# Two-layer attention and MLP kernel: the first MLP's inner sum moved from VectorE to TensorE, output biases from GpSimd to TensorE

## The reference, cut to what matters

```python
def _L0_ffn_ref(x, Win, bin_, W1, b1, W2, b2, Wout, bout):     # M = 64, INNER = 16
    s = jnp.einsum('btd,dm->btm', x, Win) + bin_
    h = jax.nn.relu(s[..., None] * W1 + b1)
    g = jnp.einsum('btmh,mh->btm', h, W2) + b2
    out = jnp.einsum('btm,md->btd', g, Wout) + bout
    return out
...
x = x + ga * _L0_attn_ref(...)
x = x + gb * _L0_ffn_ref(h, ...)          # bias bout
x = x + ga * _L1_attn_ref(h, ..., L1_attn_bo)   # bias bo
x = x + gb * _L1_ffn_ref(h, ..., L1_ffn_b2)     # bias b2
```

## Time and profile before

| what | before |
|---|---|
| time, median of 3 runs | 4289.97 us (4288.56 to 4294.81) |
| the profiled execution, first to last instruction | 4290.7 us |
| PE busy | 3633.3 us, 85% |
| PE weight loads busy | 2042.8 us, 48% |
| DVE busy | 2510.6 us, 59% |
| ACT busy | 1932.9 us, 45% |
| POOL busy | 1495.8 us, 35% |
| mean granted clock of PE | 0.914 of full |

### The profile page before, as it was taken

The page is one execution under the profiler, slowest core; times in us unless marked ns, Lnnn a source line. Parts: engine busy times, 40 slices in busy tenths (PEclk is TensorE's granted clock), DMA queues, the critical chain, the costliest instruction groups (busy, mean ns, idle before and its releaser), DMA issues. The chain is left out here.

```text
span 4290.7 us, 59366 instructions
## 1 busy us (share of the span) xinstructions
PE 3633.3 (85%) x19241; PEld 2042.8 (48%) x19241; DVE 2510.6 (59%) x6732; ACT 1932.9 (45%) x4521; POOL 1495.8 (35%) x1807
## 2 busy tenths in 40 slices
PE   7378779987899879998799978998899988998787
PEld 2245444554446534465445544465444644455433
DVE  6754757366663667446573666536674575736652
ACT  5123435545254444554355542544445543545433
POOL 4133441254323451234422543234512444235311
PEclk8589899999899989997999988999899988999888
DMA  6210230002300231002300023002310023001120
GB/s 233 70 33 13 58 104 14 13 27 56 92 16 22 53 81 42 14 12 60 102 14 24 21 55 87 15 22 53 88 34 15 12 60 102 14 24 30 46 65 6
DMA packets 230687, 203.85 MB, mean 48 GB/s; under 512 B 11457, under 2 KB 212417, under 8 KB 230346
## 3 DMA queue, kind: packets, MB, share of 16 engines
q1 hardware_dynamic: 226338, 190.51, 15.9%
q0 software_dynamic: 3328, 8.39, 0.7%
q10 hardware_dynamic: 720, 1.15, 0.1%
HBM read 121.73 MB, written 77.69 MB: 46 GB/s over the span
## 5 line engine op out<-in xcount | busy, mean ns | idle before, releaser
L2330 ACT ACTIVATE arena<-pb 128x512 f32<-128x512 f32 (+3 forms) x1536 | 671.5, 491 | 342.6 <-PE pb L1565 337.5
L2410 POOL TENSOR_TENSOR arena<-arena,small 128x512 f32<-128x512 f32 x256 | 288.0, 1127 | 463.4 <-DVE small L1740 462.0
L2159 ACT ACTIVATE arena<-arena,small 128x256 f32<-128x256 f32 x512 | 256.0, 500 | 394.9 <-DVE small L1723 388.3
L2574 POOL TENSOR_SCALAR_AFFINE_SELECT arena<-arena 128x256 f32<-128x256 f32 x512 | 220.5, 433 | 544.7 <-ACT arena L2330 542.6
L1582 PE MATMUL pb<-arena,v 128*17 128x512 f32 (+3 forms) x3072 | 365.7, 506 | 32.9 <-POOL arena L2574 24.1
L2014 DVE TENSOR_REDUCE arena<-pb 128x1 f32<-128x512 f32 x512 | 329.8, 682 | 90.6 <-PE pb L1540 89.7
L1565 PE MATMUL pb<-arena 98*128 98x512 bf16 (+3 forms) x1152 | 355.3, 343 | 9.4 <-ACT arena L2330 5.7
L1723 DVE CUSTOM_DVE_ANT_0 arena<-pb,wmask 128x256 f32<-128x256 f32 x512 | 195.8, 419 | 218.5 <-PE pb L1282 218.3
L1282 PE MATMUL pb<-arena 128*128 128x256 f32 x1024 | 283.0, 401 | 5.4 <-issue 4.0
L1259 PE MATMUL pb<-hTf,wqkv 128*128 128x512 f32 (+1 forms) x640 | 245.8, 536 | 22.6 <-DVE hTf L1692 10.8
L1660 PE MATMUL pb<-xh,w1T 128*128 128x512 f32 x512 | 251.8, 640 | 9.7 <-DVE xh L1880 8.6
(11 more groups left out here) (354 smaller groups left out, 7588.8 us busy)
## 6 DMA issues: line engine op xcount, KB each, us to landing
arena<-split_q SPq DMA_DIRECT2D x64, 384.0 KB, 4.3
arena<-split_k SPq DMA_DIRECT2D x24, 768.0 KB, 7.1
split_q<-arena SPq DMA_DIRECT2D x64, 192.0 KB, 2.3
split_q<-arena SPq DMA_DIRECT2D x96, 128.0 KB, 2.0
split_k<-arena SPq DMA_DIRECT2D x64, 192.0 KB, 2.4
split_k<-arena SPq DMA_DIRECT2D x96, 128.0 KB, 2.1
arena<-split_k SPq DMA_DIRECT2D x24, 384.0 KB, 5.7
xn<-h_d SPq DMA_DIRECT2D x8, 1024.0 KB
```

The costliest lines, as they stand in the source:

```text
L2159: ins = s.activation(pm[n % 3][:, j], sm[n % 2][:, j], ACT.Exp, bias=nmx[:, 2 * sl + j:2 * sl + j + 1], scale=-1.0, accum_out=sml[:, 2 * s ...
L2330: s.activation(pp[pn % 4][:, h % 2, 0:w_], bank[n % 3][:, 0:w_], ACT.Exp).then_inc(a_exp1, 1)
L2410: g.tensor_tensor(pm[n % 3], pm[n % 3], rcl[:, 2 * sl:2 * sl + 2].unsqueeze(2).broadcast_to([P, 2, 2 * P]), ALU.mult).then_inc(p_norm0, 1)
L2574: g.affine_select(out=p2, in_=p2, pattern=[[0, 2], [1, P]], compare_op=ALU.is_ge, fill=0.0, base=0, channel_multiplier=-1).then_inc(p_tri, 1)
```

## The change

It does five things. The diff below is cut to its core, in the order setup, PE, DVE, ACT, POOL.

1. A constant `w2d` holds eight diagonal 128 x 128 matrices, one for each column of W2. PE multiplies them with the eight Relu results and sums in PSUM (line 1497 of the changed kernel); ACT takes the sum out with the bias b2 (`gt`, line 2312). Lane buffers `rl` grow from two to eight. The eight multiply-adds and the fill of gT on DVE are gone. ACT issues two Relu in a step.
2. A chain has 36 steps in place of 42: four for the sum in place of eight and more, and behind the projection to v six steps in place of eight before the transposes.
3. The biases bout, bo and b2 enter through an extra matmul that starts the group: `ones3` (three rows of ones) times `biasw`, the bias in three bfloat16 parts. There are 2 in each chain, 4 in each `att` half and 4 in each `mlp1` half. The bias additions on POOL are gone.
4. The setup gains their making on POOL: `w2d`, and three parts of 128 x 768 values with copies, subtractions and masks, ahead of the power for the layernorm of sample 0; and one transfer.
5. `PACE` of `att(b, 0)` rises from 1.79, 0.9, 0.72 to 2.09, 1.05, 0.84 steps a round. The mask `wmask` becomes bfloat16.

```diff
-    "hrows": 16, "heavy": 58, "chain": 42, ("mlp1", 0): 24, ("mlp1", 1): 24, "hnorm": 10,
+    "hrows": 16, "heavy": 58, "chain": 36, ("mlp1", 0): 24, ("mlp1", 1): 24, "hnorm": 10,
-PACE = {('light', 0): (1.88, 0.9), ('light', 1): (1.0, 1.1), ('att', 0): (1.79, 0.9, 0.72), ('att', 1): (1.0, 1.15, 0.72)}
+PACE = {('light', 0): (1.88, 0.9), ('light', 1): (1.0, 1.1), ('att', 0): (2.09, 1.05, 0.84), ('att', 1): (1.0, 1.15, 0.72)}
...
+                g.tensor_tensor(w2d[:, :, :], ident[:, :].unsqueeze(1).broadcast_to([P, INNER // 2, P]),
+                                cols[:, C_W2:C_W2 + INNER // 2].unsqueeze(2).broadcast_to([P, INNER // 2, P]), ALU.mult).then_inc(p_w2d, 1)
+                g.wait_ge(in_bias, 16)
+                for k in range(3):
+                    if k:
+                        g.wait_ge(p_part, 2 * k)
+                    g.tensor_copy(bias_part[k], bias_raw).then_inc(p_part, 1)
+                    g.wait_ge(p_part, 2 * k + 1)
+                    g.tensor_tensor(bias_raw, bias_raw, bias_part[k], ALU.subtract).then_inc(p_part, 1)
+                g.wait_ge(p_part, 6)
+                for k in range(3):
+                    g.tensor_tensor(bias_part[k], bias_part[k], ident[:, k:k + 1].broadcast_to([P, 3 * D]), ALU.mult).then_inc(p_part, 1)
...
+                g.tensor_tensor(bw, bias_part[0], bias_part[1], ALU.add).then_inc(p_part, 1)
+                g.tensor_tensor(bw, bw, bias_part[2], ALU.add).then_inc(p_part, 1)
...
                 for _ in gpsimd_hnorm(g)(0, 0):
                     pass
...
-                    for _ in range(9):
-                        yield
+                    yield
+                    bk = chain_bank(c, j, "g")
+                    for k in range(INNER // 2):
+                        t.wait_ge(a_chain[j], nth(CHAIN_A, n, f"l{k}"))
+                        mm = t.matmul(bank[bk][:, 0:2 * P], w2d[:, k, :], L.rl[k], start=k == 0, stop=k == INNER // 2 - 1)
+                        if k == INNER // 2 - 1:
+                            mm.then_inc(t_chain[j], 1)
+                            left[bk] = [(a_chain[j], nth(CHAIN_A, n, "gt"))]
+                        if k % 2:
+                            yield
...
-                    t.wait_ge(v_chain[j], nth(CHAIN_V, n, "g8"))
+                    t.wait_ge(a_chain[j], nth(CHAIN_A, n, "gt"))
                     for i in range(2):
-                        mm = t.matmul(bank[bk][:, i * D:(i + 1) * D], L.gT[:, i * P:(i + 1) * P], wfo[:, :], start=True, stop=True)
+                        t.matmul(bank[bk][:, i * D:(i + 1) * D], ones3[:, :], biasw[:, ROW_BOUT, :], start=True, stop=False)
+                        mm = t.matmul(bank[bk][:, i * D:(i + 1) * D], L.gT[:, i * P:(i + 1) * P], wfo[:, :], start=False, stop=True)
...
-                    for _ in range(8):
+                    for _ in range(6):
                         yield
...
+                        t.matmul(bank[bk][:, 0:D], ones3[:, :], biasw[:, ROW_BO, :], start=True, stop=False)
+                        t.matmul(bank[bk][:, 0:D], ones3[:, :], biasw[:, ROW_B2, :], start=True, stop=False)
...
-                    v.tensor_copy(L.gT, cols[:, C_B2:C_B2 + 1].broadcast_to([P, 2 * P])).then_inc(done, 1)
-                    for k in range(INNER // 2):
-                        v.wait_ge(a_chain[j], nth(CHAIN_A, n, f"l{k}"))
-                        v.wait_ge(done, nth(CHAIN_V, n, f"g{k}"))
-                        v.scalar_tensor_tensor(out=L.gT, in0=L.rl[k % 2], scalar=cols[:, C_W2 + k:C_W2 + k + 1], in1=L.gT,
-                                               op0=ALU.mult, op1=ALU.add).then_inc(done, 1)
+                    for _ in range(8):
                         yield
                     scale(0)
-                    yield
                     add(1)
                     yield
                     scale(1)
-                    yield
...
-                        if k >= 2:
-                            s.wait_ge(v_chain[j], nth(CHAIN_V, n, f"g{k - 1}"))
-                        s.activation(L.rl[k % 2], L.sT, ACT.Relu, scale=cols[:, C_W1 + k:C_W1 + k + 1], bias=cols[:, C_B1 + k:C_B1 + k + 1]).then_inc(done, 1)
-                        yield
+                        s.activation(L.rl[k], L.sT, ACT.Relu, scale=cols[:, C_W1 + k:C_W1 + k + 1], bias=cols[:, C_B1 + k:C_B1 + k + 1]).then_inc(done, 1)
+                        if k % 2:
+                            yield
+                    s.wait_ge(t_chain[j], nth(CHAIN_T, n, "g"))
+                    s.activation(L.gT, bank[chain_bank(c, j, "g")][:, 0:2 * P], ACT.Identity, bias=cols[:, C_B2:C_B2 + 1]).then_inc(done, 1)
+                    yield
...
-                g.tensor_tensor(x, x, bias.unsqueeze(1).broadcast_to([P, 2, D]), ALU.add).then_inc(done, 1)
-                    add_bias(b, c, rows[:, R_B2:R_B2 + D], gates[:, 3])
```

More of the change, by code:

```diff
@@ L45 @@
 NCOLS = 40
-R_NULL, R_BOUT, R_BO, R_B2 = (i * D for i in range(4))
-R_GB = 4 * D
+R_NULL, R_GB = 0, D
 NROWS = R_GB + 4 * HD1
+ROW_BOUT, ROW_BO, ROW_B2 = range(3)
 UNITS = TH * H0 // 2
@@ L145, in turn @@
             return
-        if key[0] == "chain" and key[2] == 3 and n == 41 and not reached([(("chain", key[1], 2), 42), (("att", key[1], 0), 22)]):
+        if key[0] == "chain" and key[2] == 3 and n == STEPS["chain"] - 1 and not reached([(("chain", key[1], 2), STEPS["chain"]), (("att", key[1], 0), 22)]):
             return
@@ L235, in chain_bank @@
     banks = CHAIN_BANKS[c, j]
-    return banks[CHAIN_T.index(op) % len(banks)]
+    turns = [o for o in CHAIN_T if o != "g"]
+    return banks[turns.index("wfo" if op == "g" else op) % len(banks)]
 def nth(ops, n, op):
@@ L369, in adaln_kernel @@
         xh = sb("xh", [P, KD * NH])
-        gbias = sb("gbias", [P, 2, D])
+        w2d = sb("w2d", [P, INNER // 2, P])
+        biasw = sb("biasw", [P, 3, D], BF16)
+        ones3 = sb("ones3", [P, P], BF16)
         small = sb("small", [P, 640])
@@ L700, in adaln_kernel @@
         wtmp = [at(arena, 16384 + F1 * i, [F1]) for i in range(2)]
+        bias_raw = at(arena, 18432, [3 * D])
+        bias_part = [at(arena, 18432 + 3 * D + 3 * D // 2 * i, [3 * D], BF16) for i in range(3)]
         TURNS = [(m, c0, min(4, BINARY[m][1] // P - c0)) for m in range(FT + KD) for c0 in range(0, BINARY[m][1] // P, 4)]
@@ L1171, in __init__ @@
                 view = zone(arena, z)
-                self.sT, self.rl, self.gT = view([2 * P]), [view([2 * P]) for _ in range(2)], view([2 * P])
+                self.sT, self.rl, self.gT = view([2 * P]), [view([2 * P]) for _ in range(INNER // 2)], view([2 * P])
                 self.xpair = view([2, D])
@@ L1672, in mlp1 @@
                                 t.wait_ge(a_g, FT * H + k + 1)
-                            mm = t.matmul(bank[bk][:, 0:D], g1[:, k, i * P:(i + 1) * P], w2T[:, k], start=k == 0, stop=k == FT - 1)
+                            mm = t.matmul(bank[bk][:, 0:D], g1[:, k, i * P:(i + 1) * P], w2T[:, k], start=False, stop=k == FT - 1)
                             if k == FT - 1:
@@ L2299, in chain @@
                     yield
-                    for _ in range(5):
+                    for _ in range(3):
                         yield
@@ L2692, in put_rows @@
                                          L.parts[i][:, m0 + m].unsqueeze(1).broadcast_to([P, n_rows, 2 * P])).then_inc(split_out[c][j], 16)
-                    for _ in range(38):
+                    for _ in range(32):
                         yield
@@ L2810 @@
         "ones": np.full((KA - KS, G1 * N), 0x3F803F80, np.uint32).view(f32),
-        "wmask": np.where(np.stack([first, band, last], 1), 0, NEG).astype(f32),
+        "wmask": (np.where(np.stack([first, band, last], 1), 0, NEG).astype(f32).view(np.uint32) >> 16).astype(np.uint16).reshape(P, 6 * P).view(f32),
         "cmask": np.where(i[None] > i[:, None], NEG, 0).astype(f32),
```

95 lines of the change are left out of this document (41 added, 54 removed).

## The result

The changed kernel took 4390.23 us (median of 4 runs, 4383.63 to 4394.87), the kernel before beside it 4290.6: a ratio of 1.0231, 95% interval 1.0217 to 1.0244. That is 99.6 us slower, where +61 was forecast. Its profiled execution has a span of 4393.1 us, which lies 2.9 us above the median (that of before lay 0.7 above).

What follows compares the result with a forecast made beforehand. PE, busy 85% of the span, was taken as the fullest engine. Terms summed to +6.2 a sample, +50 over eight, plus setup +11: +61 on 4290.7, giving 4351 us, range 4255 to 4415.

Steps and rivals of the forecast that it cites:

- D: Before the first fill: PE's wait for split q and k goes, 58 us in all, about 7.3 a sample.
- C: Second window-attention half: diagonals and bias rows less filled waits, +6.7 a sample; PE waiting at the chains' tails, net +9.7.
- The sign of being right: PE's wait for the last rotation step before the chain's transposes rises from 22.4 to over 100 us, nearly all beside window attention.
- A: Diagonal matmuls in the chains: 512 records at 0.226, 116 us of PE, 14.5 a sample, half beside the window attention.
- E: First half of layer-1 attention: added PE work against waits for DVE and low-clock time given back, net -4.5 a sample.
- B: Bias rows: 192 bfloat16 matmuls at 0.13 us on PE, 25 us, 3.1 a sample.
- F: Elsewhere: 12 bias rows a sample in the MLP halves and second attention half, where PE is full, +1.6.
- G: Setup, once: POOL's new work of 22.3 us delays the layernorm's power, which DVE awaits, +11 us.
- Split k still awaited (D fails): Sign of being wrong: PE still waits for split k at the first fill, so D fails.
- Rival one: The clock comes back in the first attention half: E is -12, C's net half, 4252 us; 20%.
- Rival two: The chains' tails are covered, DVE being less slowed by POOL: C's net about 2, 4290 us, no change; 13%.
- Rival three: PE pays in full in the first attention half, low clock staying: E is +8.2, 4453 or about 4400 us; 15%.

Runs made afterwards that it cites:

- Run 1: Changed kernel, but SyncE starts the loads of split q and k after the window attention's last scores, not its last output product: 4341.13 us.
- run 2: Kernel before the change, with SyncE's loads of split q and k started after the window attention's last scores: 4267.62 us.
- Run 3: Changed kernel with the two steps between v and the chain's transposes restored (chains of 38 steps): 4335.63 us.
- run 4: Changed kernel with the inner sum on DVE again, chains of 42 steps, old pace; bias rows, setup and bfloat16 mask kept: 4304.54 us.
- run 6: Changed kernel, chains 0 and 1 summing on DVE (42 steps), chains 2 and 3 on PE (38), early loads, POOL's setup work behind the power: 4266.62 us.

## Why the prediction was right, and where it was not

The direction, the stated range, and the case that was given 52% (4310 to 4410) were right. The size was 39 us short, and one term of the sum was off by more than that.

**D failed.** The forecast took away 7.3 us a sample at the first fill because the stores come sooner. They do: the last one is issued 26.4 us ahead of the fill where it was 20.2. But the prediction read who was late (the load of split k) and then asked what comes before it in the data, the stores, instead of what the issue itself waited for. The issue times decide: 2484.00 in the kernel before, at the end of the last L1313, 14 us behind the last store. Run 1 shows the cause, run 2 that the same holds before the change. The stretch to the fill went from 10.4 to 10.6: an error of 7.5 a sample, 53 in seven. In the first sample, where the stores are late, the step was right (22.8 to 10.5), and that sample came out at -2.5 instead of +6.2.

**C, the tail, was right** in mechanism and nearly in size. PE stood still for 7.04 us against 7.8 at chain 0, and for 3.54 behind it, where 2.3 was forecast. PE's idle time in the second half rose by 8.3 us a sample; the forecast's +9.7, less the 1.0 of small waits filled, is 8.7. Run 3 gives back 6.6 in that half, and 1.5 in the attention half, where the forecast had no such term. The sign of being right was read from a wrong row: the 22.4 us are 8.4 for the last rotation step (L1967) and 13.9 for L1984, which empties the bank of the transposes. The wait for the rotation went from 8.4 to 88.9, 82.7 of it beside the window attention, where over 100 was named.

**A was right in size and wrong in place.** Chain 0's diagonal matmuls stand in the first half, not the second: PE has 16 of their records (3.9 us) there. Hence +4.2 in the first half, which was forecast to gain only bias rows, and +11.9 in the second instead of 16.4. By run 4 against run 3 the sum costs 7.4 in both, against the 7.2 less 1.0 of the forecast.

**E** came out at -2.7 instead of -4.5. PE's idle time there fell by 4.5 (17.0 to 12.5), where 5.7 was forecast. Its busy time rose by 1.8, where +8.2 - 7 was: the time at the low clock fell from 28.9 to 22.0 us a sample, which at half speed is some 3.5, half of the 7 that I gave back for it, and 8 of the diagonal records stand ahead of the fill. The reason given, DVE's relief from 16 multiply-adds, is right in part at most. Run 4 has the full 2.7 with all of them still on DVE, 2.3 of idle time among it. What relief and pace gave beyond that (2.2 more of idle time, and the low clock from 27.0 to 22.0) paid for the diagonal matmuls there and no more. **B and F** were somewhat high: a row costs 0.11, not 0.13, and about half of them are covered.

**G** was +11 and measured +5.3. In POOL's timeline of the changed kernel the power stands at 163.00, where the earlier trace rows have 156.57:

```profile
162.53 0.40 POOL L1057 TENSOR_TENSOR ones<-ones,ident 128x128 bf16<-128x128 bf16 x1
163.00 1.04 POOL L773 TENSOR_TENSOR small<-small,mhalf 128x4 f32<-128x4 f32 x1
```

That is 6.4 later, not 11: the new work took 19.1 us and not 22.3 (two of the three casts over 128x768 took 0.82 us, the width gave 1.76), and began 1.4 earlier. DVE waited 3.5 of it; most of the rest is DVE slowed beside POOL (L907, 2.4 us more in its four instructions), which the forecast did not have.

Added up, 7 x 14.1 - 2.5 + 5.3 = 101.5 is the difference of the spans, 102.4, within the rounding. Against the forecast the seven samples are 55 us over, of which D is 53; the first sample is 9 and the setup 6 under. That the terms without D sum to +13.5 a sample and measured 13.9 is partly luck: by stretches they were off by +3.7 in the first half, -4.5 in the second, +1.8 in the attention and -0.6 in the rest.

Of the other signs named, the second half grew to 106.9 and not 112, PE's busy time by 93.6 and not 130, and the clock of the attention half stayed under 0.9 (0.86 in the fifth sample, 0.88 over seven, from 0.85 and 0.84). "Split k still awaited (D fails)" is the sign that came true.

Rival one (the clock comes back) did not happen in full, as this clock shows. The rule cited from the Trainium skill for it (TensorE: Matmul & The Clock Gate, HAM oscillation) could be tried by run 1, which has no gap before the fills: the time at the low clock in the attention half falls from 22.0 to 16.0 us a sample, in the direction of the rule. In run 2 the same gap was closed and it rose from 28.9 to 32.4. So these runs do not show that the gap is the cause. Rival two's lock agrees with rows of the setup; in the attention half it is not shown (run 4). In the tail the scaling and addition of the rotation fell from 1028 and 1412 ns on average (2419.3 to 2440 us of the kernel before) to 674 and 1051 (2466.8 to 2490 of the changed one), but the product before them rose from 678 to 950, which leaves 0.9 us in two halves; the stretch between v and the transposes is 14.7 us, longer than the 13.3 of the forecast. Rival three did not happen.

## What to carry to other kernels

When a transfer is what ends a wait, look up when it was issued and which event its issue followed, before you reason about its data; here one semaphore, for a product that has nothing to do with the buffer, cost 27 us in one kernel and 49 in the other. Steps in an order written by hand are distances: the spacing between a serial chain on one engine and its consumer on another must be kept or measured when steps elsewhere are taken out, since those two steps cost 54 us, more than the 33 by which run 3 stands above run 4. And work moved to the fullest engine can pay only in a stretch where that engine stands idle; here nothing came of it even there until the order was tightened, and whether tightening alone would have done it was not tried.

## What the runs showed of the hardware

- DVE was slowed beside POOL in the setup: tensor_scalar over 128x256 took 890 ns on average in run 6 and 407 in the kernel before, where POOL was nearly idle, and an int32 operation over 128x4 took 556 against 162.
- A bfloat16 bias row over 128x256 takes 0.11 us of PE when it is issued in a run of matmuls, half of a float32 record (0.226).
- The 7.05 us from the end of the last output product to the first fill are the way of the loads: the first issue at 2541.98, split k (384 KB) issued at 2543.04, the fill at 2549.03. Stores that end earlier did not shorten it. With the issue at 2500.86, 12.8 us ahead of that product's end, the fill waited for nothing in run 1.
